# Gathers of four tiles ahead in one unrolled block, with the spread, the masks and an addition moved off GpSimd

## The reference, cut to what matters

```
x = x + einsum('bct,bcd->bdt', x, w0[cond])          # a 32x32 matrix of 200 per sequence
x = x + attention(x)                                 # below
x = x + x @ W_base^T + scaling[a] * lora(x; A[a], B[a], Wt, Wp)   # one of 4 adapters
x = x + einsum('bct,bcd->bdt', x, w3[subject])       # a 32x32 matrix of 8 per sequence
```

```
k_blocks = k_blocks.at[blk, :, off, :].set(k); v_blocks = ...
allowed = (kpos <= pos) & (kpos > pos - 128)
p = softmax(where(allowed, q @ k_all^T * SCALE, -inf));  o = p @ v_all;  out = o @ Wo^T
```

## Time and profile before

| what | value |
|---|---|
| median of 3 runs | 302.19 us (301.96 to 303.79) |
| the profiled run | 302.65 us, its span 300.8 us |
| TensorE busy | 210.8 us, 70% of the span |
| VectorE busy | 209.0 us, 69% |
| GpSimd busy | 164.2 us, 55% |
| ScalarE busy | 131.8 us, 44% |
| mean granted clock of TensorE | 0.905 of full |

### The profile page before, as it was taken

The page is one execution under the profiler, slowest core; times in us unless marked ns, Lnnn a source line. Parts: engine busy times, 40 slices in busy tenths (PEclk is TensorE's granted clock), DMA queues, the critical chain, the costliest instruction groups (busy, mean ns, idle before and its releaser), DMA issues.

```text
span 300.8 us, 7985 instructions
## 1 busy us (share of the span) xinstructions
PE 210.8 (70%) x2402; PEld 155.9 (52%) x2402; DVE 209.0 (69%) x628; ACT 131.8 (44%) x491; POOL 164.2 (55%) x279
## 2 busy tenths in 40 slices
PE   0132599699899993005788876897868879988773
PEld 0112475455555551004667755675657667767641
DVE  0987947888699985204589876784884867878760
ACT  0220015155444553321756664465555744667510
POOL 4456856067555557754266666556656665673120
PEclk9999859799999998555799998997997998999998
DMA  5819995034611000023031434233424343331011
GB/s 151 258 34 209 211 381 112 17 107 136 194 55 46 29 20 35 32 64 97 4 111 55 118 89 129 73 110 93 142 58 113 95 128 74 115 104 58 20 37 35
DMA packets 18319, 29.70 MB, mean 99 GB/s; under 512 B 8189, under 2 KB 13640, under 8 KB 17906
## 3 DMA queue, kind: packets, MB, share of 16 engines
q0 software_dynamic: 7408, 19.04, 22.9%
q1 hardware_dynamic: 8130, 5.22, 6.0%
q10 hardware_dynamic: 2752, 5.08, 5.4%
HBM read 29.43 MB, written 7.34 MB: 122 GB/s over the span
## 4 chain that ended last, share of the span: by engine, by line
issue 28%; POOL 24%; PE 19%; DMA 16%; DVE 4%; POOLq 4%; ACT 3%; SPq 0%; ACTq 0%; DVEq 0%
DMA big<-in_pool,row_now 4%; DMA w0c<-in_w,w_i 4%; PE quad L1119 4%; POOL own L547 4%; PE quad L1171 4%; POOL big L482 3%; POOL work L504 3%; PE bank L1157 3%; POOL big L542 3%; DMA merged<-work,row_now 2%; POOLq L422 2%; POOL merged L517 2%; DMA big<-merged,row_now 2%; POOL w0c L436 2%; DMA con<-in_consts 2%
## 5 line engine op out<-in xcount | busy, mean ns | idle before, releaser
L699 ACT ACTIVATE work<-bank,nmx 128x164 f32<-128x164 f32 x128 | 49.6, 398 | 30.3 <-DVE nmx L981 24.7
L1157 PE MATMUL bank<-kt_rope,big 128*128 128x164 f32 x256 | 46.8, 319 | 0.0
L1157 PEld LDWEIGHTS bank<-kt_rope,big 128*128 128x128 f32 x256 | 43.4, 205 | 5.0 <-issue 0.8
L995 DVE TENSOR_TENSOR onT<-quad,rT 32x256 f32<-32x256 f32 x64 | 26.9, 420 | 21.9 <-PE quad L1171 20.4
L1153 PE MATMUL bank<-mask,identb 128*128 128x492 bf16 (+1 forms) x48 | 18.2, 379 | 30.3 <-DVE kt_rope L972 22.7
L981 DVE TENSOR_REDUCE nmx<-bank 128x3 f32<-128x492 f32 (+1 forms) x48 | 28.5, 593 | 12.3 <-PE bank L1157 12.1
L1119 PE MATMUL quad<-wqkv_sb,work 128*128 128x512 f32 x64 | 34.2, 660 | 2.8 <-ACT work L652 2.7
L988 DVE STREAM_TRANSPOSE work<-work 128x768 f32<-128x768 f32 (+2 forms) x96 | 34.7, 410 | 0.0
L682 ACT ACTIVATE big<-qT,con 128x256 f32<-128x256 f32 (+1 forms) x64 | 27.2, 512 | 0.1
L517 POOL DMA_INDIRECT merged<-work,row_now x16 | 18.3, 1141 | 15.4 <-ACT work L646 9.0
L436 POOL DMA_INDIRECT w0c<-in_w,w_i x16 | 16.9, 1054 | 17.9 <-DMA w0c<-in_w,w_i 7.1
(11 more groups left out here) (158 smaller groups left out, 469.6 us busy)
## 6 DMA issues: line engine op xcount, KB each, us to landing
merged<-big ACTq DMA_DIRECT2D x3, 1024.0 KB
xin<-in_x SPq DMA_DIRECT2D x16, 128.0 KB
out<-x4s SPq DMA_DIRECT2D x16, 128.0 KB, 2.0
w3bd<-in_w SPq DMA_DIRECT2D x64, 4.0 KB
con<-in_consts SPq DMA_DIRECT2D x1, 660.5 KB, 5.2
wqkv_sb<-in_wqkv ACTq DMA_DIRECT2D x1, 512.0 KB
wt_sb<-in_wt ACTq DMA_DIRECT2D x1, 256.0 KB
wp_sb<-in_wp ACTq DMA_DIRECT2D x1, 256.0 KB
```

The source lines that it names most:

```text
L699: act.activation(prob[:, p, hd, 0:NK], ps_sc[(p + i) % 2][:, j * NK:j * NK + NK], ACT.Exp, bias=nmx[:, p, hd:hd + 1], scale=1.0, accum_out ...
L995: ve.tensor_tensor(onT[rows, :, :].rearrange("p c (b n) -> p b c n", b=NB), ps_o[rows, :, 64 * (g % 2):64 * (g % 2) + 64].rearrange("p b ( ...
L1157: mm = pe.matmul(at[:, j * NK:j * NK + NK], qbd[:, p, hd, :], kT[:, p, hd // GSZ, 0:NK], start=False, stop=(j == n - 1), skip_group_check= ...
```

## The change

- The copies of indices into `row_now` go, except that of the scatter: the gathers read `idx` directly, since GpSimd's part of phase 2 is unrolled and the tile is a constant there. So the waits for descriptors after each gather go as well.
- GpSimd's phase 2 is new: `fetch` for tiles 0 to 3 first, then for each step zm of tile s-2, and for tile s+3 the cached gather once the weighted sums of tile s-1 are done, and `fetch`. Within `fetch` the own gather comes first, then the wait for the cached one to land, then the merged gather.
- The spread of the reciprocals moves to ScalarE, one instruction of 128x256 behind the x4s copy and ahead of the first exponents.
- The masks of all 16 tiles are made once by VectorE, as 0 and 1, just before the first `keys`; `identb` holds the large negative number on its diagonal.
- The identity is added once to all 8 matrices of w3 (VectorE, at the start), and the result is written to DRAM by SyncE, from where it is loaded per tile. SyncE's wait for `w3i_done` becomes one for `l3_done`.

```diff
+            sp.dma_start(w3e[:, :, :], w3.rearrange("n c d -> c n d")).then_inc(s_w3e, 16)
...
+            sp.wait_ge(w3e_done, 1)
+            sp.dma_start(w3_d.rearrange("n c d -> c n d"), w3e[:, :, :]).then_inc(s_w3d, 16)
+            sp.wait_ge(s_w3d, 16)
...
                     if reused(t):
-                        sp.wait_ge(w3i_done, t - 1)
-                    diagonal(t, p, w3, subj_sb, w3bd, s_w3)
+                        sp.wait_ge(l3_done, t - 1)
+                    diagonal(t, p, w3_d, subj_sb, w3bd, s_w3)
...
             def cached(t, r):
-                pl.tensor_copy(row_now[:, 0, r:r + 1], idx[:, 0, bass.ds(t, 1)]).then_inc(row4_copied, 1)
-                wait(row4_copied, t + 1)
                 pl.indirect_dma_start(
                     out=kvb[:, r, :], out_offset=None, in_=pool_rows4,
-                    in_offset=bass.IndirectOffsetOnAxis(ap=row_now[:, 0, r:r + 1], axis=0),
+                    in_offset=bass.IndirectOffsetOnAxis(ap=idx[:, 0, t:t + 1], axis=0),
                     bounds_check=4 * NPOOL - 1, oob_is_err=False, engine_sem=desc_cache).then_inc(s_cache[r], 16)
-                wait(desc_cache, t + 1)
-            def masks(t, p):
...
             def fetch(t, r, n):
-                pl.tensor_copy(row_now[:, 1:3, r:r + 1], idx[:, 1:3, bass.ds(t, 1)]).then_inc(rowm_copied, 1)
-                wait(rowm_copied, t + 1)
+                pl.indirect_dma_start(
+                    out=own[:, r, :], out_offset=None, in_=merged_rows2,
+                    in_offset=bass.IndirectOffsetOnAxis(ap=idx[:, 2, t:t + 1], axis=0),
+                    bounds_check=SEGS * 8 - 1, oob_is_err=False, engine_sem=desc_fetch).then_inc(s_own[r], 16)
                 wait(s_cache[r], 16 * (n + 1))
                 pl.indirect_dma_start(
                     out=kvb[:, r, :], out_offset=None, in_=merged_rows4,
-                    in_offset=bass.IndirectOffsetOnAxis(ap=row_now[:, 1, r:r + 1], axis=0),
+                    in_offset=bass.IndirectOffsetOnAxis(ap=idx[:, 1, t:t + 1], axis=0),
                     bounds_check=SEGS * 4 - 1, oob_is_err=False, engine_sem=desc_fetch).then_inc(s_merge[r], 16)
-                wait(desc_fetch, 2 * t + 1)
...
+            for t in range(RING):
+                fetch(t, t, 0)
+            for s in range(NT + 2):
+                t = s - 2
                 if valid(t):
                     wait(zs_done, t + 1)
-                    if not isinstance(t, int) or t >= 1:
+                    if t >= 1:
                         wait(l2_done, t)
                     pl.tensor_tensor(zm[0:E * R, :].rearrange("p (b c) -> p b c", b=NB),
...
-                    pl.tensor_tensor(w3i[:, p, :], w3bd[:, p, :], ident, ALU.add).then_inc(w3i_done, 1)
...
+                t = s - 1
+                if valid(t) and valid(t + RING):
+                    wait(pv_done, t + 1)
+                    cached(t + RING, t % RING)
+                    fetch(t + RING, t % RING, t // RING + 1)
...
-            act.copy(identb[:, :], ident).then_inc(s_prec, 1)
+            act.activation(identb[:, :], ident, ACT.Copy, scale=NEG).then_inc(s_prec, 1)
...
+                if valid(t1):
+                    act.wait_ge(rden_done, t1 + 1)
+                    if not isinstance(t1, int) or t1 >= 1:
+                        act.wait_ge(rT_done, t1)
+                    act.copy(rwide[:, :].rearrange("p (c g d) -> p c g d", c=GSZ, g=G),
+                             rden[:, 1 - p, :].rearrange("p (g c) -> p c g", c=GSZ).unsqueeze(3)
+                             .broadcast_to([128, GSZ, G, HD])).then_inc(rwide_done, 1)
...
+            ve.wait_ge(s_w3e, 16)
+            ve.tensor_tensor(w3e[:, :, :], w3e[:, :, :], cc("ident", TOK)[:, 0:TOK].unsqueeze(1)
+                             .broadcast_to([TOK, 8, TOK]), ALU.add).then_inc(w3e_done, 1)
...
+            for k, (name, a, b, op) in enumerate((("backpos", 0, NKB, ALU.is_lt), ("ownpos", NKB, NK, ALU.is_gt))):
+                ve.tensor_tensor(mask[:, :, a:b], cc(name).unsqueeze(1).broadcast_to([128, NT, b - a]),
+                                 pos3[:, k, :].unsqueeze(2).broadcast_to([128, NT, b - a]), op).then_inc(mask_done, 1)
             keys(0, 0, 0, 0)
...
-                    pe.wait_ge(mask_done, 2 * (t + 1))
+                    pe.wait_ge(mask_done, 2)
...
-                    pe.matmul(ps_l3, w3i[:, 1 - p, :], x3s[:, 1 - p, :], start=True, stop=True).then_inc(l3_done, 1)
+                    pe.matmul(ps_l3, w3bd[:, 1 - p, :], x3s[:, 1 - p, :], start=True, stop=True).then_inc(l3_done, 1)
```

More of the change, by code:

```diff
@@ L188, in build @@
         kT = kt_rope[:, 0:2 * G * KW].rearrange("p (a g k) -> p a g k", a=2, g=G)
-        mask = sb("mask", [128, 2, NK], BF16)
+        mask = sb("mask", [128, NT, NK], BF16)
         work = sb("work", [128, 7008])
@@ L346, in build @@
         on_used = sem("on_used")
[L347 removed]
+        s_blank = sem("s_blank")
+        s_w3e, w3e_done, s_w3d = sem("s_w3e"), sem("w3e_done"), sem("s_w3d")
         pT_done, pv_done, rden_done = sem("pT_done"), sem("pv_done"), sem("rden_done")
@@ L517, in phase1 @@
                     pl.indirect_dma_start(
-                        out=merged, out_offset=bass.IndirectOffsetOnAxis(ap=row_now[:, 3, r:r + 1], axis=0),
+                        out=merged, out_offset=bass.IndirectOffsetOnAxis(ap=row_now[:, r:r + 1], axis=0),
                         in_=kvrow[:, r, :], in_offset=None,
@@ L523, in phase1 @@
                     cached(4 * h + u - 4, u % RING)
-                if isinstance(h, int) and NT <= 4 * h + u < NT + 2:
-                    masks(4 * h + u - NT, u % 2)
             steps(pl, phase1, *P1)
@@ L572, in phase2 @@
                                      zs[:, :].rearrange("p (b c) -> p b c", b=NB),
-                                     zscale[:, bass.ds(t * NB, NB)].unsqueeze(2).broadcast_to([E * R, NB, TOK]),
+                                     zscale[:, t * NB:t * NB + NB].unsqueeze(2).broadcast_to([E * R, NB, TOK]),
                                      ALU.mult).then_inc(zm_done, 1)
-                    wait(s_w3[p], 64 * (k + 1))
-                    if reused(t):
-                        wait(l3_done, t - 1)
-                    pl.tensor_tensor(w3i[:, p, :], w3bd[:, p, :], ident, ALU.add).then_inc(w3i_done, 1)
-                t, k, p, r, n = at_step4(h, u, -1)
-                if valid(t) and reused(t):
-                    wait(sc_done, 3 * (t - 1))
-                    masks(t, p)
-                t, k, p, r, n = at_step4(h, u, -2)
-                if valid(t):
-                    fetch(t, r, n)
-                t, k, p, r, n = at_step4(h, u, -3)
-                if valid(t) and (not isinstance(t, int) or t >= RING):
-                    wait(pv_done, t - 3)
-                    cached(t, r)
-            steps(pl, phase2, NT + 2, *P2R[1:])
+                t = s - 1
[3 more added lines that the diff above has]
+                    fetch(t + RING, t % RING, t // RING + 1)
         @block.scalar
@@ L1009, in phase2 @@
                     ve.wait_ge(exp_done, H * (t1 + 1))
+                    if reused(t1):
+                        ve.wait_ge(rwide_done, t1 - 1)
                     ve.reciprocal(rden[:, p1, :], den[:, p1, :]).then_inc(rden_done, 1)
@@ L1153, in scores @@
                 pe.matmul(at[:, 0:n * NK], identb[:, :],
-                          mask[:, p, :].unsqueeze(1).broadcast_to([128, n, NK]), start=True, stop=False,
+                          mask[:, bass.ds(t, 1), :].broadcast_to([128, n, NK]), start=True, stop=False,
                           skip_group_check=True)
```

39 lines of the change are left out of this document (7 added, 32 removed).

## The result

| | before | after |
|---|---|---|
| median | 302.31 us (301.96 to 303.79, 4 runs) | 280.56 us (279.48 to 280.89, 4 runs) |
| ratio, 95% interval | | 0.9266 [0.9226, 0.9305] |
| profiled run, its span | 302.65, 300.8 us | 279.48, 277.1 us |
| granted clock of TensorE, mean | 0.905 | 0.924 |

The forecast was 279 us, in a range of 273 to 288. Every ratio in this document leaves out runs that lie more than 1.5% above the fastest one of the same kernel. The same two views are read first. The first is the changed kernel's page: busy time by engine, and the chain that ended last by engine.

What follows compares the result with a forecast made beforehand. GpSimd's turn of 10.0 us a step was taken as the bound. Terms -20.4 - 3.3 - 1.0 - 0.8 + 0.4 + 2.0 = -23.1 us turned the 302.19 us median into 279.1, said as 279, range 273 to 288.

Steps and rivals of the forecast that it cites:

- The steps: Attention steps 1 to 14: GpSimd leaves the path, 7.9 us a step, 102.7 against 123.06 us, -20.4 us.
- rival E: Attention steps: descriptor waits weren't the cost, dropping them alone brings nothing; inside the forecast, no chance of its own.
- Descriptor waits, "I take nothing": Gaps of 0.84 us ahead of gathers: any shrinking is off the path; bounds nothing and 0.84 for each gather.
- (a): End of the projections: two sets of masks leave GpSimd's chain, where scatters wait behind them, -3.3 us.
- (b): End of the projections: four cached gathers lose their index copy, -1.0 us, bounds nothing and 1.5.
- (c): Ahead of the steps: VectorE adds the identity to w3 once, on the way to GpSimd's row lists, +0.4 us.
- (e): Last scatter: VectorE's mask operation shuts GpSimd's index copy out of SBUF, +2.0 us, bounds nothing and 2.8.
- (f): Prologue: the fourth gather VectorE needs before its first maxima comes earlier, gain 0.3 to 1.8, taken as -0.8 us.
- A: GpSimd still sets the period: a landing of 5.5 us gives 8.8 a step, 290 us; chance 0.12.
- B: TensorE's clock still drops to the lower level in the steps, 13 x 1.0 us, 292 us; chance 0.05.
- C: SyncE's stores, behind the w3 loads, come late: 8.5 us a step, 287 us; chance 0.05.
- D: Slower than before: GpSimd waits for late cached-gather landings; 6.5 us uses up the gain, 8.1 gives 321 us; chance 0.02.

Runs made afterwards that it cites:

- b2: The kernel before with only the masks made once on VectorE instead of in GpSimd's steps: 299.44 us, ratio 0.9827.
- c2: The kernel before with masks made once on VectorE and the own gather issued ahead of the wait for the cached gather's landing: 285.64 us, ratio 0.9415.
- a4: The changed kernel with the spread of the reciprocals back on GpSimd, behind the wait for the cached gather's landing: 300.14 us, ratio 0.9861.
- c3: The changed kernel with the spread of the reciprocals back on GpSimd, ahead of the wait for the cached gather's landing: 281.77 us, ratio 0.9277.
- a3: The changed kernel with the three waits for descriptors after the gathers put back: 279.99 us, ratio 0.9218.
- b1: The kernel before with only the three descriptor waits of the attention steps dropped: 294.61 us, ratio 0.9712.
- a1: The changed kernel with VectorE's mask operations waiting until the last scatter's descriptors are written: 279.41 us, ratio 0.9206.
- c1: The changed kernel with VectorE's masks held until the last scatter's descriptors are written and SyncE's store issued ahead of the w3 loads: 277.31 us, ratio 0.9181.
- a2: The changed kernel with SyncE issuing a tile's store ahead of the w3 loads, not behind them: 279.72 us, ratio 0.9229.
- a5: The changed kernel with two of ScalarE's four query copies left out from the third tile on: 284.24 us, ratio 0.9348.

## Why the prediction was right, and where it was not

- **The steps.** Forecast 7.9 us each and -20.4 in all; measured 7.92 and -20.1. GpSimd left the path in the way written out there: cached gather, own gather inside the landing, wait, merged gather, zm. Its turn was put at 7.7 us, and from the end of one tile's weighted sums (186.75) to the end of zm (194.49) it is 7.74. The landing was 4.5 us as a median (4.3 to 5.0). The gap that shrank, ahead of the own gather, lies inside the landing; the two that count, behind the weighted sums and behind the landing, did not. So the room is the 0.2 us of the forecast, and not the 1.1 us that GpSimd waits.
- **What carries it.** Right in the sum, wrong in a sentence: rival E says that the forecast "lives from work moved off GpSimd". b2 moves most of that work and brings 1.7%; c2 adds only an order, and brings 4% more; a4 and c3 differ by order alone, 5.8%. What the change does is to empty the cycle from weighted sums through the cached gather's landing to what TensorE needs next. Work taken from an engine counts only where it is on that cycle, and the masks of the earlier trace rows lay in the landing.
- **Descriptor waits, "I take nothing".** The 0.84 us do shrink, to 0.30: 0.54 of it was the wait, inside the bounds of nothing and 0.84. Off the path in the changed order, as said (a3, no difference). In the kernel before it was on the path: b1, -2.9%, the most of the three single edits. So rival E's "dropping them alone brings nothing" was wrong, and the sign that the forecast had named for it, gaps well under 0.84 us, did come.
- **The spread on ScalarE, cost nothing.** It takes 0.40 us, in ScalarE's idle time ahead of the exponents. Right, and it is needed only because of the place (a4, c3).
- **(a), (b), (c).** The scatter before the last one started at 120.54 for 124.76 us: -4.2, where -3.3, -1.0 and +0.4 were forecast, -3.9. The part with the masks, between the 13th and the 15th of the 16 scatters, fell by 2.9 us (114.82 to 124.76 before, 113.51 to 120.54 now) for the 3.3 of (a). Up to the 13th it was 1.3, where (b) and (c) give 0.6. The +0.4 of (c) doesn't show: the first scatter is 0.2 us later (60.29, now 60.50), and as late in b1 and b2, which don't have that addition.
- **(e), the lock.** +2.0 forecast, 2.1 measured (2.27 us for 0.18), and shown by a1.
- **(f), the prologue.** From the last scatter to VectorE's second large transpose it was 12.8 us (127.06 to 139.85) and is 11.4 (124.68 to 136.06): -1.4, where -0.8 was forecast. Both of its terms were off, to opposite sides:

```profile
132.01 1.01 POOL L534 DMA_INDIRECT big<-merged,idx  x1 [0.30 <-issue]
...
136.06 0.71 DVE L945 STREAM_TRANSPOSE kt_rope<-big 128x512 f32<-128x512 f32 x1 [1.21 <-DMA big<-merged,idx]
```

  The fourth gather starts 7.33 us behind the last scatter (124.68 to 132.01), where it was 9.27 (127.06 to 136.33): 1.9 us gained for a forecast of 0.3, mostly because three gaps of 0.77 to 0.80 us ahead of gathers are now 0.30. But VectorE gets it 4.05 us after its start, where it was 3.52 and less had been expected: 0.5 us lost. So the forecast for (f) was near by two errors of opposite sign. Of the 3.8 us that the second transpose is then ahead in all, step 0's weighted sums keep 3.1; VectorE's first maxima now wait 0.22 us for TensorE's scores.
- **Not forecast.** Step 0 to 1 is 1.3 us shorter. The tail is 0.8 us longer, and this is TensorE's clock: four products (L1178) in the changed kernel, at a granted clock of 0.52 (268.8 to 271.0), and the same four (L1179) in c1, at 1.00 (267.1 to 268.3), each in its tail. In the kernel before they took 1.13 us too.

```profile
268.81 2.05 PE L1178 MATMUL bank<-wob,onT 128*128 128x256 f32 x4 [0.46 <-ACT x4s L672]
```

```profile
267.13 1.13 PE L1179 MATMUL bank<-wob,onT 128*128 128x256 f32 x4 [0.46 <-ACT x4s L672]
```

- **The rivals.** A did not come; zm is just in time (TensorE's loads wait for it 6 times, 0.2 us at most). B did not come: the clock is 1.00 from step 1 to 14. C came twice, with waits of up to 1.9 us where the sum had 0.8 at the worst, so the margin of that queue is thinner than it said; in the profile of c3, its longest run, it came three times with 9.2 us in all. Its 8.3 us doesn't follow from its own terms either: 4.17 and 3.7 are 7.9, and 8.7 with the 0.8 to wake up. a2 closes it. D did not come: landings stay at 5.0 us and below.
- **The total.** That the profiled run's 279.48 us meets a forecast of 279.5 is luck in part: it was the fastest of four. By the ratio the change saves 22.2 us for a forecast of 23.1, and the 1.3 us of step 0 to 1, which no term had, stand against the tail's 0.8 and the smaller misses above.

## What to carry to other kernels

Before counting how much work an engine is relieved of, lay out the closed cycle that sets the period, with the transfer's landing in it, and ask on which side of each wait an instruction stands: the same 0.5 us cost 18 us behind the landing wait and nothing ahead of it. When work is taken from an engine that waits for a landing, look at whether it was filling that wait; if so, move an independent issue into the hole in the same edit. A one-off operation that moves to VectorE is still not free for GpSimd while it runs, so put it where GpSimd waits for a transfer.

## What the runs showed of the hardware

- A GpSimd copy that takes 0.18 us took 2.27 us when a VectorE operation with two SBUF inputs had begun 0.03 us ahead of it (the changed kernel and a1), and beside such an operation a gather's instruction took 1.57 us instead of 1.06 (a1).
- Consecutive indirect transfers of GpSimd stand 0.30 us apart without a wait between them, 0.77 to 0.84 us with a wait for the descriptors, and 0.77 to 0.86 us behind a copy of the index.
- 512 KB of cached rows landed 4.3 to 5.0 us after the start of the gather in the changed kernel, with a share of the DMA engines of 0.39.
- The weighted sums of TensorE can take 0.5 us longer at the same clock, for no cause that the profile names (2.16 for 1.68 us, a5).
